# Softmax attention in a four-layer kernel on one core: the order of score and weighing matmuls, and the width of the maxima

## The chip, the cores and the metric

The kernel runs on one core of a Trainium2 chip. The metric is the device time of one execution in microseconds, median of the runs shown.

## What is computed

The reference is a chain of four layers on 1024 tokens of width 256: layer norm and softmax attention with 16 heads, a mixture of 8 experts, a linear attention with 16 heads, and a second mixture. The change touches the softmax attention alone. Cut to that:

```python
Xn = (X - mu) * rsqrt(var + 1e-5) * ln_w + ln_b        # 1024 x 256
q, k, v = split(Xn @ W_in)                              # 16 heads of 16 channels
q, k = rope(q), rope(k)                                 # the first 8 channels of each head
p = softmax(q @ k.T * 16 ** -0.5)                       # 16 x 1024 x 1024
context = p @ v                                         # then @ W_out, and the residual
```

## The kernel before, in words

Everything stands in one program. `attention_block` is its first block: a preparation (norm, transposes, tables of the rotary embedding, the projections of the first group of four heads and of all values), and then a loop over *units*. Each of the five engines runs its own instruction list in order, and semaphores tie them together.

A head's queries and keys lie in `q_stack` and `k_stack` as three float32 parts of 16 channels each, 48 rows, once on partitions 0 to 63 and once on 64 to 127 (`side` 0 and 1; `q_stack` holds another half of the queries on each side). Two more rows carry the negated row maximum, so that the second product comes out shifted.

- `score_rows_q(g, side)`: one matmul of 48 rows gives 128 queries x 512 keys. DVE (`row_maxima`) takes its maximum over the 512 keys. A head has 8 units (`NT`), of two such matmuls each, one per side; two halves of the keys are combined at the head's end (`whole_max`). Three banks of PSUM, `ps_q`, go round.
- POOL splits the maxima in two parts (`split_maxima`), PE turns them (`turn_max`), ACT copies them (`copy_max`), and SP's queue writes them into `q_stack`.
- `score_rows_k(kk, side)`: one matmul of 50 rows gives 128 keys x 512 queries, already shifted by the maximum; ACT takes the exponential into `probs` (`exp`). Three banks, `ps_k`, go round. It runs `K_LAG` = 13 units behind the maxima.
- `weigh(w)`: every second unit, two key tiles are weighed with the values (16 channels and a one for the sum, padded to 32 columns). Four matmuls of 128 x 32 weights and 512 moving columns write four strips of 32 partitions of one bank, `ps_ctx`: two strips for the even key tiles, two for the odd. In float32 each matmul is two instructions in the profile.
- When a head is done, ACT copies the bank (`copy_ctx`), PE turns its four blocks of 128 (`turn_ctx`, two and two) into `ps_turn`, ACT takes them (`take_ctx`), POOL adds the strips of even and odd tiles (`add_ctx`), DVE inverts the sums (`norm_ctx`), POOL multiplies (`weigh_ctx`).

The queries and keys of the other three groups of heads are projected inside the loop in 12 pieces of 256 columns (`project_piece`, units 0 to 11), copied by ACT (`copy_piece`), partly swapped by DMAs from SP's queue (`swap`), and prepared by POOL (`prepare`). `EARLY_AT` puts the projection of the first half of the contexts into the loop's tail. The functions `rotate`, `low`, `split_early` and all blocks behind attention are not edited.

A unit's order on PE is: `score_rows_q(g, 0)` with `score_rows_k(kk, 1)`, then perhaps a turn, then `score_rows_k(kk, 0)` with `score_rows_q(g, 1)`, then perhaps a piece, then on every second unit `weigh`. Two score matmuls on different sides run side by side in the array; such two are called a pair below.

## Time and profile before

| what | value |
|---|---|
| median of 3 runs | 1087.62 us |
| lowest, highest | 1085.27, 1093.72 us |
| the profiled execution, first to last instruction | 1084.3 us |
| mean granted clock of TensorE in it | 0.982 |
| PE busy | 1028.1 us (95%) |
| DVE busy | 787.5 us (73%) |
| ACT busy | 673.7 us (62%) |
| POOL busy | 507.1 us (47%) |

The profiled execution is given by its span; the fastest run stands 1.0 us above that and the median 3.3, which is what lies around a span and what runs differ by. PE's busy time counts matmuls as pipelined, so a high share says only that some matmul was under way. PE in a row is the matmul, PEld the load of its weights, SPq and ACTq are issues of DMAs. PEclk is the clock granted to TensorE, 1.00 being 2.4 GHz and 0.50 being 1.2 GHz.

### The profile page before, as it was taken

The page shows a single profiled execution, that of the slowest core. Times are in us where ns is not written, and L with a number is a line of the kernel's source. Part 1 is how long each engine was busy: PE and PEld are TensorE (multiplying, and loading weights), DVE is VectorE, ACT ScalarE, POOL GpSimd, SP SyncE. Part 2 cuts the span into 40 slices and gives each one's busy share as a digit, 9 for nine tenths or more (in the row PEclk, how much of TensorE's full clock was granted, in tenths as well). Part 3 has the DMA queues.
Part 4 walks back from the last instruction along what each step waited for, and adds up shares of the span by engine and source line. Part 5 has one row for each costly group of instructions (what it writes and reads, how often), then busy time and mean ns, then how long its engine had stood idle before and what let it go on. Part 6 is the DMA issues. An engine that isn't in the chain of part 4 may idle for free. (4 is left out here: it accounts for less than half of the span.)

```text
span 1084.3 us, 18619 instructions
## 1 busy us (share of the span) xinstructions
PE 1028.1 (95%) x6437; PEld 812.5 (75%) x6437; DVE 787.5 (73%) x1789; ACT 673.7 (62%) x1235; POOL 507.1 (47%) x457
## 2 busy tenths in 40 slices
PE   7999999989999997799999999999889999999997
PEld 5433333347888986699988998899789778888997
DVE  5789999836766856898999999998567465333843
ACT  4478888756544447788778878787456344333454
POOL 3252331114058561767686777777506000536544
PEclk9989999999999998899999999999899999999999
DMA  4533434205224300351113121221011123655100
GB/s 91 91 64 56 76 54 68 70 13 164 78 70 136 49 2 23 113 181 64 55 64 113 59 65 54 93 73 39 2 36 28 44 57 88 159 159 163 67 20 21
DMA packets 80633, 79.28 MB, mean 73 GB/s; under 512 B 29320, under 2 KB 67676, under 8 KB 80540
## 3 DMA queue, kind: packets, MB, share of 16 engines
q1 hardware_dynamic: 80228, 77.66, 27.0%
q8 instruction: 52, 0.85, 0.3%
q10 hardware_dynamic: 312, 0.43, 0.3%
q14 instruction: 41, 0.34, 0.1%
HBM read 65.51 MB, written 1.28 MB: 62 GB/s over the span
## 5 line engine op out<-in xcount | busy, mean ns | idle before, releaser
L682 ACT ACTIVATE attn_probs<-attn_rows_k 128x512 f32<-128x512 f32 x256 | 134.4, 605 | 37.2 <-PE attn_rows_k L533 37.0
L770 DVE TENSOR_REDUCE attn_row_max<-s_sum 128x1 f32<-128x512 f32 x171 | 111.8, 682 | 15.9 <-PE s_sum L519 13.3
L533 PE MATMUL attn_rows_k<-attn_q_stack,attn_k_stack 50*128 50x512 f32 x256 | 96.9, 465 | 5.7 <-ACT attn_probs L682 5.6
L2865 DVE TENSOR_TENSOR late_mids<-late_mids,late_bank 128x512 f32<-128x512 f32 (+1 forms) x50 | 34.4, 687 | 78.8 <-PE late_bank L67 75.8
L65 PE MATMUL late_bank<-net_x_part_low,late_w_T 128*128 128x512 f32 (+1 forms) x192 | 77.9, 406 | 0.0
L66 PE MATMUL late_bank<-net_x_part_low,late_w_T 128*128 128x512 f32 (+1 forms) x192 | 76.1, 396 | 0.0
L67 PE MATMUL late_bank<-net_x_part_low,late_w_T 128*128 128x512 f32 (+1 forms) x192 | 76.0, 396 | 0.0
L519 PE MATMUL s_sum<-attn_k_stack,attn_q_stack 48*128 48x512 f32 x171 | 72.8, 470 | 1.9 <-DMA attn_q_stack<-s_part 1.4
L1530 POOL TENSOR_TENSOR gold_mids<-gold_mids,s_later 128x512 f32<-128x512 f32 x32 | 51.9, 1659 | 46.2 <-DMA s_later<-gold_weights 46.2
L2770 ACT ACTIVATE late_mids<-late_bank 128x512 f32<-128x512 f32 (+1 forms) x50 | 29.9, 597 | 69.6 <-PE late_bank L67 69.5
L2966 POOL TENSOR_TENSOR late_mids<-late_mids,late_raw_w_T_last 128x512 f32<-128x512 f32 x22 | 29.8, 1378 | 89.7 <-DMA late_raw_w_T_last<-top_weights 89.7
L547 PE MATMUL attn_ctx<-attn_probs,attn_v 128*32 128x512 f32 x512 | 69.9, 619 | 0.0
L2119 DVE SCALAR_TENSOR_TENSOR lin_conv_q<-lin_pair,early_lin_taps,lin_conv_q 128x1021 f32<-128x1021 f32 (+2 forms) x48 | 61.5, 1281 | 7.3 <-ACT lin_conv_q L1979 4.0
L2119 DVE SCALAR_TENSOR_TENSOR lin_conv_k<-lin_pair,early_lin_taps,lin_conv_k 128x1021 f32<-128x1021 f32 (+2 forms) x48 | 61.4, 1279 | 2.7 <-issue 0.4
L770 DVE TENSOR_REDUCE attn_row_max<-attn_rows_q 128x1 f32<-128x512 f32 x85 | 57.9, 682 | 6.7 <-PE attn_rows_q L519 4.2
L519 PEld LDWEIGHTS s_sum<-attn_k_stack,attn_q_stack 48*128 48x128 f32 x171 | 30.3, 189 | 42.9 <-DVE attn_row_max L770 31.5
L533 PEld LDWEIGHTS attn_rows_k<-attn_q_stack,attn_k_stack 50*128 50x128 f32 x256 | 42.0, 189 | 24.2 <-ACT attn_probs L682 22.9
L1864 PE MATMUL lin_pair<-lin_probs,lin_v_rows 128*128 128x128 f32 x256 | 48.3, 282 | 4.3 <-DVE lin_state L2111 4.3
L1988 ACT ACTIVATE lin_normed_k<-lin_pair,lin_k_shift,lin_rstd_k 128x128 f32<-128x128 f32 x128 | 46.3, 473 | 0.6 <-DVE lin_k_shift L2091 0.6
L65 PE MATMUL late_bank<-late_down_T,late_w_T 128*128 128x256 f32 (+1 forms) x152 | 43.3, 285 | 1.8 <-POOL late_w_T L2565 1.8
L2755 ACT ACTIVATE late_w_T<-late_mids 128x256 fp32r<-128x256 f32 (+3 forms) x57 | 27.4, 488 | 27.4 <-PE late_bank L67 27.4
L1867 PE MATMUL lin_pair<-lin_q_dec,lin_state 128*128 128x128 f32 x224 | 44.3, 280 | 0.0
(459 smaller groups left out, 3491.9 us busy)
## 6 DMA issues: line engine op xcount, KB each, us to landing
lin_mix<-decay_sums SPq DMA_DIRECT2D x16, 512.0 KB, 3.8
lin_q_dec<-decay_sums SPq DMA_DIRECT2D x16, 512.0 KB, 5.3
s_later<-gold_weights SPq DMA_DIRECT2D x16, 256.0 KB, 3.6
attn_k_stack<-s_part SPq DMA_DIRECT2D x30, 128.0 KB, 3.5
s_raw_ring<-in_L_ffn_Wg SPq DMA_DIRECT2D x12, 256.0 KB, 2.8
s_raw_ring<-in_L_ffn_Wu SPq DMA_DIRECT2D x12, 256.0 KB, 3.1
attn_q_stack<-s_part SPq DMA_DIRECT2D x32, 64.0 KB, 2.4
gold_raw_w_down<-in_L_ffn_Wd SPq DMA_DIRECT2D x1, 2048.0 KB, 12.9
```

The source lines that it names most:

```text
L65: pe.matmul(out, w[0], x[0], start=start, stop=False)
L66: pe.matmul(out, w[0], x[1], start=False, stop=False)
L67: return pe.matmul(out, w[1], x[0], start=False, stop=stop)
L519: pe.matmul(ps_q[n % 3][:, :], q_stack[rows, h % SLOTS, r * P:(r + 1) * P], k_stack[rows, h % SLOTS, half * HALF:(half + 1) * HALF], start ...
L533: pe.matmul(ps_k[n % 3][:, :], k_stack[rows, h % SLOTS, t * P:(t + 1) * P], q_stack[rows, h % SLOTS, :], start=True, stop=True).then_inc(s ...
L547: i = pe.matmul(ps_ctx[j * VW:(j + 1) * VW, :], v[:, 2 * p + odd, h, :], probs[:, (2 * w + odd) % PB, b * HALF:(b + 1) * HALF], start=(p = ...
L682: act.activation(probs[:, kk % PB, side * HALF:(side + 1) * HALF], ps_k[n % 3][:, :], ACT.Exp)\
L770: dve.tensor_reduce(row_max[:, tile, half:half + 1], ps_q[n % 3][:, :], axis=AX, op=ALU.max)\
L1530: pool.tensor_tensor(out, out, weight[v % 4], ALU.mult).then_inc(weighted, 1)
L1864: i = pe.matmul(pair[2][:, cols], self.v_rows[h // 2 % 2][:, c, h % 2, :], self.probs[:, c, :], start=True, stop=(c == 0))
L1988: i = act.activation(self.normed[1][:, c, :], self.tiled[2][:, c, :], ACT.Identity, scale=self.rstd[1][:, c:c + 1], bias=self.k_shift[:, c ...
L2119: i = dve.scalar_tensor_tensor(self.conv[m][:, back:T], self.pair[pair][:, 0:T - back], self.taps[:, m, h, j:j + 1], self.conv[m][:, back: ...
```

## The change

The loop goes by *rounds* of two units, 4 per head, `ROUNDS_ALL` = 74 in all.

- **Maxima.** A tile of 128 queries x 1024 keys now fills two neighbouring banks, and DVE takes one maximum over the 1024 columns. Two pairs of banks alternate (a third serves in the first six rounds). `whole_max` and its combination are gone.
- **Order of the scores.** In a round PE does `score_rows_q` of side 0 for both halves of the keys, paired with `score_rows_k` of side 1 for two key tiles; then the same with the sides exchanged. Scores with the maximum lag 7 rounds, weighing 8.
- **Weighing.** `weigh(w, odd)` takes one key tile at a time: four matmuls of 32 weight columns and 256 moving columns, one for each quarter of the queries, into four strips of one half bank. It stands twice in a round, once behind each two pairs. Even and odd tiles accumulate in the same strips, so `add_ctx` is gone, `copy_ctx` copies 256 columns instead of 512, and one turn of two blocks replaces two turns.
- **Banks.** `ps_turn` is gone. The turns, the pieces and the exponentials share a ring of three banks, in an order computed beforehand (`ring`).
- **Pieces.** Six pieces of 512 columns instead of twelve of 256, one in each of rounds 0 to 5.
- **Queues.** The DMAs that write the rows of minus one and the first two swaps are issued by ACT instead of SP.

The core of the diff:

```diff
-        whole_max = [s.sb(f"whole_max{b}", [P, NT]) for b in range(2)]
+        row_max = [s.sb(f"row_max{b}", [P, NT]) for b in range(2)]
...
+        ctx_T = [s.sb(f"ctx_T{b}", [P, QUARTER]) for b in range(2)]
+        whole, inv = s.sb("whole", [P, 2, 2, 4, CW]), s.sb("inv", [P, 2, 2, 4])
...
+        ps_k = [ps_pair2[:, n * HALF:(n + 1) * HALF] for n in range(2)] + [s.ps("rows_k2", [P, HALF])[:, :]]
         ps_ctx = s.ps("ctx", [P, HALF])
-        ps_turn = s.ps("turn", [P, HALF])
-        turn_max_ps = ps_turn[0:MROWS * NT, 0:P]
-        piece_ps = ps_turn[:, 0:HALF // 2]
+        sums = ps_ctx[:, 0:QUARTER]
...
         inner = probs[:, 0:2, :].rearrange("p a (c d) -> p (a c) d", d=D)
         rope_rows = [probs[:, 2 + n, :].rearrange("p (c d) -> p c d", c=NT) for n in range(2)]
...
+        ROUNDS = NT // 2
+        Q_ROUNDS = ROUNDS * NH
+        K_LAG, W_LAG = 7, 8
+        MAX_LAG, COPY_LAG, TURN_LAG, NORM_LAG = ROUNDS, W_LAG + ROUNDS, W_LAG + ROUNDS + 1, W_LAG + ROUNDS + 2
+        ROUNDS_ALL = ROUNDS * (NH - 1) + TURN_LAG + 1
+        PIECES = 6
...
-        EARLY_AT = {UNITS + 1: ("turn", 0), UNITS + 2: ("rows", 0), UNITS + 3: ("rows", 1),
-                    UNITS + 4: ("project", 0), UNITS + 5: ("project", 1), UNITS + 7: ("turn", 1)}
-        def units():
-            for g in range(SLOTS_ALL * NT):
-                kk = g - K_LAG
-                w = kk - W_LAG
-                yield (g // NT, g % NT, g if g < UNITS else None, kk if 0 <= kk < UNITS else None,
-                       w // 2 if w % 2 and 0 < w < UNITS else None)
+        EARLY_AT = {Q_ROUNDS: (("turn", 0),), Q_ROUNDS + 1: (("rows", 0), ("rows", 1)),
+                    Q_ROUNDS + 2: (("project", 0), ("project", 1)), Q_ROUNDS + 3: (("turn", 1),)}
+        def rounds():
+            for q in range(ROUNDS_ALL):
+                k, w = q - K_LAG, q - W_LAG
+                yield (q, q if q < Q_ROUNDS else None, k if 0 <= k < Q_ROUNDS else None, w if 0 <= w < Q_ROUNDS else None)
...
+        def tile_bank(n):
+            return n % 3 if n < 2 * PIECES else n % 2
...
+        K_SIDES = ((0, 1), (1, 1), (0, 0), (1, 0))
+        ring = []
+        for q, _, k, _ in rounds():
+            if k is not None:
+                ring += [("exped", 4 * k + 1), ("exped", 4 * k + 2)]
+            if head_at(q, TURN_LAG) is not None:
+                ring.append(("ctx_taken", head_at(q, TURN_LAG) + 1))
+            if k is not None:
+                ring += [("exped", 4 * k + 3), ("exped", 4 * k + 4)]
+            if q < PIECES:
+                ring.append(("piece_copied", q + 1))
+            if head_at(q, MAX_LAG) is not None:
+                ring.append(("max_copied", head_at(q, MAX_LAG) + 1))
...
+        def ring_bank(job):
+            n = ring.index(job)
+            return ps_k[2 if n < ring_first else (n - ring_first) % 3]
...
-                def project_piece(n, r):
-                    first = n % 2 * HALF + r * HALF // 2
...
+                def project_piece(n):
+                    if n == 0:
                         pe.wait_ge(rest_loaded, 64)
-                    else:
-                        pe.wait_ge(piece_copied, 2 * n + r)
-                    if 2 * n + r == FIRST_TURN:
-                        pe.wait_ge(max_copied, 1)
-                    project(piece_ps, w_qk[:, :, 1 + n // 2, :], slice(first, first + HALF // 2)).then_inc(pieced, 1)
+                        pe.wait_ge(v_copied, 4)
+                    out = ring_free(("piece_copied", n + 1))
+                    project(out, w_qk[:, :, 1 + n // 2, :], slice(n % 2 * HALF, (n % 2 + 1) * HALF)).then_inc(pieced, 1)
...
-                def score_rows_q(g, side):
-                    h, u = divmod(g, NT)
-                    r, half = divmod(u, 2)
-                    if u == 0 and side == 0:
...
+                    if half == 0 and tile_before[n] is not None:
+                        pe.wait_ge(maxed, tile_before[n] + 1)
                     rows = slice(side * SIDE_ROWS, side * SIDE_ROWS + QROWS)
-                    pe.matmul(ps_q[n % 3][:, :], q_stack[rows, h % SLOTS, r * P:(r + 1) * P],
+                    pe.matmul(ps_tile[tile_bank(n)][:, half * HALF:(half + 1) * HALF],
+                              q_stack[rows, h % SLOTS, r * P:(r + 1) * P],
                               k_stack[rows, h % SLOTS, half * HALF:(half + 1) * HALF], start=True, stop=True)\
                         .then_inc(scored_q, 1)
...
-                def score_rows_k(kk, side):
-                    h, t = divmod(kk, NT)
-                    if t == 0 and side == 1:
...
-                    n = 2 * kk + 1 - side
-                    if n >= 3:
-                        pe.wait_ge(exped, n - 2)
+                            pe.wait_ge(maxed, 2 * PIECES)
+                    out = ring_free(("exped", 4 * k + n + 1))
                     rows = slice(side * SIDE_ROWS, side * SIDE_ROWS + QROWS + MROWS)
-                    pe.matmul(ps_k[n % 3][:, :], k_stack[rows, h % SLOTS, t * P:(t + 1) * P], q_stack[rows, h % SLOTS, :],
+                    t = 2 * r + odd
+                    pe.matmul(out, k_stack[rows, h % SLOTS, t * P:(t + 1) * P], q_stack[rows, h % SLOTS, :],
                               start=True, stop=True).then_inc(scored_k, 1)
...
-                def weigh(w):
-                    h, p = divmod(w, NT // 2)
-                    pe.wait_ge(exped, 4 * (w + 1))
-                    if p == 0 and h >= 1:
+                def weigh(w, odd):
+                    h, r = divmod(w, ROUNDS)
+                    t = 2 * r + odd
+                    pe.wait_ge(exped, 4 * w + 3 + odd)
+                    if t == 0 and h >= 1:
                         pe.wait_ge(ctx_copied, h)
-                    for odd in range(2):
-                        for b in range(2):
-                            j = 2 * b + odd
-                            i = pe.matmul(ps_ctx[j * VW:(j + 1) * VW, :], v[:, 2 * p + odd, h, :],
-                                          probs[:, (2 * w + odd) % PB, b * HALF:(b + 1) * HALF],
-                                          start=(p == 0), stop=(p == NT // 2 - 1))
+                    for j in range(4):
+                        i = pe.matmul(sums[j * VW:(j + 1) * VW, :], v[:, t, h, :],
+                                      probs[:, (2 * w + odd) % PB, j * QUARTER:(j + 1) * QUARTER],
+                                      start=(t == 0), stop=(t == NT - 1))
                     i.then_inc(summed, 1)
...
-                for n, u, g, kk, w in units():
-                    if u == U_MAX and 1 <= n <= NH:
-                        turn_max(n - 1)
-                    if g is not None:
-                        score_rows_q(g, 0)
-                    if kk is not None:
-                        score_rows_k(kk, 1)
-                    if u in U_CTX and 3 <= n:
-                        turn_ctx(n - 3, U_CTX.index(u))
-                    if kk is not None:
-                        score_rows_k(kk, 0)
-                    if g is not None:
-                        score_rows_q(g, 1)
-                    if n * NT + u in PIECE_AT:
-                        project_piece(*PIECE_AT[n * NT + u])
+                for n, q, k, w in rounds():
+                    if k is None and q is not None:
+                        for half in range(2):
+                            for side in range(2):
+                                score_rows_q(q, side, half)
+                    if k is not None:
+                        for p in range(2):
+                            if q is not None:
+                                score_rows_q(q, 0, p)
+                            score_rows_k(k, p)
                     if w is not None:
-                        weigh(w)
-                    if n * NT + u in EARLY_AT:
-                        what, j = EARLY_AT[n * NT + u]
+                        weigh(w, 0)
+                    if head_at(n, TURN_LAG) is not None:
+                        turn_ctx(head_at(n, TURN_LAG))
+                    if k is not None:
+                        for p in range(2):
+                            if q is not None:
+                                score_rows_q(q, 1, p)
+                            score_rows_k(k, 2 + p)
+                    if w is not None:
+                        weigh(w, 1)
+                    if n < PIECES:
+                        project_piece(n)
+                    if head_at(n, MAX_LAG) is not None:
+                        turn_max(head_at(n, MAX_LAG))
+                    for what, j in EARLY_AT.get(n, ()):
                         {"turn": turn_early, "rows": add_rows, "project": project_early}[what](j)
-                for half in range(2):
-                    turn_ctx(NH - 1, half)
...
-                    act.activation(plain_half(n)[:, r * HALF // 2:(r + 1) * HALF // 2], piece_ps, ACT.Copy)\
-                        .then_inc(piece_copied, 1)
+                    act.activation(plain_half(n), ring_bank(("piece_copied", n + 1)), ACT.Copy).then_inc(piece_copied, 1)
...
                 def copy_ctx(h):
-                    act.wait_ge(summed, NT // 2 * (h + 1))
+                    act.wait_ge(summed, NT * (h + 1))
...
-                    act.activation(ctx_T[h % 2][:, :], ps_ctx[:, :], ACT.Copy).then_inc(ctx_copied, 1)
+                        act.wait_ge(ctx_turned, h - 1)
+                    act.activation(ctx_T[h % 2][:, :], sums, ACT.Copy).then_inc(ctx_copied, 1)
...
-                def exp(kk):
-                    if kk >= PB:
-                        act.wait_ge(summed, (kk - PB) // 2 + 1)
-                    for side in (1, 0):
-                        n = 2 * kk + 1 - side
-                        act.wait_ge(scored_k, n + 1)
-                        act.activation(probs[:, kk % PB, side * HALF:(side + 1) * HALF], ps_k[n % 3][:, :], ACT.Exp)\
-                            .then_inc(exped, 1)
+                    view = ring_bank(("ctx_taken", h + 1))[:, 0:2 * P].rearrange("p (c s w) -> p c s w", c=2, s=4)
+                    act.activation(whole[:, h % 2, :, :, :], view[:, :, :, 0:CW], ACT.Copy).then_inc(ctx_taken, 1)
+                def exp(k, n):
+                    odd, side = K_SIDES[n]
+                    if n < 2 and 2 * k + odd >= PB:
+                        act.wait_ge(summed, 2 * k + odd - PB + 1)
+                    act.wait_ge(scored_k, 4 * k + n + 1)
+                    act.activation(probs[:, (2 * k + odd) % PB, side * HALF:(side + 1) * HALF],
+                                   ring_bank(("exped", 4 * k + n + 1)), ACT.Exp).then_inc(exped, 1)
...
-                for n, u, g, kk, w in units():
-                    if u == U_MAX and 1 <= n <= NH:
-                        copy_max(n - 1)
-                    if u == U_COPY and 2 <= n < NH + 2:
-                        copy_ctx(n - 2)
-                    if kk is not None:
-                        exp(kk)
-                    if u == U_TAKE and 3 <= n:
-                        take_ctx(n - 3)
-                    if n * NT + u in PIECE_AT:
-                        copy_piece(*PIECE_AT[n * NT + u])
-                    if n == 0:
-                        norm_x(u)
-                take_ctx(NH - 1)
+                stack_ones()
+                for n, q, k, w in rounds():
+                    if head_at(n, COPY_LAG) is not None:
+                        copy_ctx(head_at(n, COPY_LAG))
+                    if k is not None:
+                        exp(k, 0)
+                        exp(k, 1)
+                    if head_at(n, TURN_LAG) is not None:
+                        take_ctx(head_at(n, TURN_LAG))
+                    if k is not None:
+                        exp(k, 2)
+                        exp(k, 3)
+                    if n < PIECES:
+                        copy_piece(n)
+                        if n < 2:
+                            act.wait_ge(piece_copied, n + 1)
+                            swap_rows(act, n)
+                    if n < ROUNDS:
+                        norm_x(2 * n)
+                        norm_x(2 * n + 1)
+                    if head_at(n, MAX_LAG) is not None:
+                        copy_max(head_at(n, MAX_LAG))
...
-                def row_maxima(g):
-                    h, u = divmod(g, NT)
...
-                    for side in range(2):
-                        n, tile = 2 * g + side, r + side * NT // 2
-                        dve.wait_ge(scored_q, n + 1)
-                        dve.tensor_reduce(row_max[:, tile, half:half + 1], ps_q[n % 3][:, :], axis=AX, op=ALU.max)\
-                            .then_inc(maxed, 1)
-                    if u == NT - 1:
-                        if h >= 2:
-                            dve.wait_ge(max_split, h - 1)
-                        dve.drain()
-                        dve.tensor_tensor(whole_max[h % 2][:, :], row_max[:, :, 0], row_max[:, :, 1], ALU.max)\
-                            .then_inc(whole_ready, 1)
-                        dve.drain()
+                def row_maxima(q, side):
+                    h, r = divmod(q, ROUNDS)
+                    n = 2 * q + side
+                    if r == 0 and side == 0 and h >= 2:
+                        dve.wait_ge(max_split, h - 1)
+                    dve.wait_ge(scored_q, 4 * (q + 1) if side or q < K_LAG else 4 * q + 2)
+                    tile = r + side * ROUNDS
+                    dve.tensor_reduce(row_max[h % 2][:, tile:tile + 1], ps_tile[tile_bank(n)][:, :], axis=AX, op=ALU.max)\
+                        .then_inc(maxed, 1)
```

## Rows read from the trace of the kernel before

**Rows 1.** stage windows; length, busy us (instructions) of each engine, PEclk, DMA share, GB/s

```profile
50.94:61.18 10.24, 10.17 (x39) 3.92 (x39) 6.93 (x13) 5.46 (x12) 6.04 (x7) 0.50 0.14 26
...
72.80:83.76 10.96, 10.63 (x71) 4.02 (x70) 10.12 (x18) 9.06 (x21) 6.58 (x9) 1.00 0.44 80
...
52.30:208.72 156.42, 151.72 (x963) 56.84 (x963) 142.32 (x251) 126.30 (x265) 44.43 (x78) 0.97 0.39 68
28.02:52.30 24.28, 22.81 (x87) 12.40 (x88) 19.45 (x32) 11.36 (x26) 6.02 (x7) 0.97 0.54 93
208.72:235.64 26.92, 23.19 (x133) 9.54 (x131) 9.61 (x15) 17.37 (x35) 5.42 (x12) 0.99 0.00 1
```

**Rows 2.** the table of waits, 72.8 to 204.4 us

```profile
PEld s_sum L519 <- DVE attn_row_max L770: 22.6, 30, 0.8
```

**Rows 3.** PE's timeline: start us, us, engine, line, operation

```profile
170.18 0.40 PE L519 MATMUL attn_rows_q<-attn_k_stack,attn_q_stack 48*128 48x512 f32 x1
...
170.51 0.44 PE L505 MATMUL attn_turn<-net_ident,attn_ctx_T 128*128 128x128 f32 x2
...
170.89 0.49 PE L519 MATMUL s_sum<-attn_k_stack,attn_q_stack 48*128 48x512 f32 x1
171.31 1.07 PE L547 MATMUL attn_ctx<-attn_probs,attn_v 128*32 128x512 f32 x8
172.30 0.49 PE L519 MATMUL s_sum<-attn_k_stack,attn_q_stack 48*128 48x512 f32 x1
...
172.64 0.40 PE L519 MATMUL attn_rows_q<-attn_k_stack,attn_q_stack 48*128 48x512 f32 x1
```

**Rows 4.** passes of 512 and 256 columns: ns min/median/max

```profile
L447 PE MATMUL attn_rows_k<-net_raw_x_part,attn_w_qk x8: 592/592/697, 11.5 to 17.4; 128*128 128x512 f32 x8
...
L468 PE MATMUL attn_rows_k<-s_raw_w_v,net_raw_x_part x16: 379/379/379, 23.0 to 26.2; 128*128 128x256 f32 x16
```

**Rows 5.** PE's timeline, a turn behind a lone score matmul

```profile
216.11 0.49 PE L533 MATMUL attn_rows_k<-attn_q_stack,attn_k_stack 50*128 50x512 f32 x1
216.53 0.44 PE L505 MATMUL attn_turn<-net_ident,attn_ctx_T 128*128 128x128 f32 x2
```

**Rows 6.** DVE on PSUM, 512 and 1024 columns: ns min/median/max

```profile
L770 DVE TENSOR_REDUCE attn_row_max<-s_sum x171: 641/681/693, 28.6 to 209.3; 128x1 f32<-128x512 f32 x171
...
L2099 DVE TENSOR_TENSOR lin_probs<-lin_pair,lin_mix x16: 1210/1211/1217, 457.0 to 781.2; 128x1024 f32<-128x1024 f32 x16
```

**Rows 7.** ACT: four exponentials in the timeline; the 256-column copy, a group's line

```profile
172.93 2.07 ACT L682 ACTIVATE attn_probs<-attn_rows_k 128x512 f32<-128x512 f32 x4 [0.63 <-PE attn_rows_k L533]
...
L656 ACT ACTIVATE s_later<-attn_turn 128x256 f32<-128x256 f32 x8 | 3.1, 385 | 7.4 <-PE attn_turn L447 7.4
```

**Rows 8.** PE's timeline, a piece's projection and the next pair

```profile
30.05 1.13 PE L447 MATMUL attn_turn<-net_raw_x_part,attn_w_qk 128*128 128x256 f32 x4
31.11 0.50 PE L519 MATMUL s_sum<-attn_k_stack,attn_q_stack 48*128 48x512 f32 x1
```

**Rows 9.** DMA issues in the timeline, on ACT's and on SP's queue

```profile
21.88 2.56 ACTq L233 DMA_DIRECT2D attn_k_stack<-s_part  x4
...
33.53 5.40 SPq L255 DMA_DIRECT2D s_raw_ring<-s_raw_ring  x4
```

**Rows 10.** PE's timeline, weighings at the beginning and in the tail

```profile
53.53 1.93 PE L547 MATMUL attn_ctx<-attn_probs,attn_v 128*32 128x512 f32 x8
...
61.87 1.06 PE L547 MATMUL attn_ctx<-attn_probs,attn_v 128*32 128x512 f32 x8
...
217.33 1.07 PE L547 MATMUL attn_ctx<-attn_probs,attn_v 128*32 128x512 f32 x8
...
221.79 0.64 PE L547 MATMUL attn_ctx<-attn_probs,attn_v 128*32 128x512 f32 x4
...
231.19 1.06 PE L547 MATMUL attn_ctx<-attn_probs,attn_v 128*32 128x512 f32 x8
```

**Rows 11.** POOL's timeline, the addition of the last context

```profile
234.14 0.43 POOL L375 TENSOR_TENSOR attn_whole<-attn_whole 128x136 f32<-128x136 f32 x1 [1.21 <-ACT attn_whole L674]
```

168 lines of the change are left out of this document (80 added, 88 removed).

## The prediction

> **What bounds the kernel now.** I read the stage windows first [rows 1]. Only the attention block is edited; its loop begins at 28.02 us and the block ends at 235.64. Everything before and behind is the same code, so the question is what the 207.6 us between become. I cut them where the change's rounds can be laid on the old units: 24.28 us until unit 16 (the first that weighs values), 156.42 for units 16 to 127, 26.92 for the tail in which maxima are finished and scores and weighing run out. In the middle piece one head (8 units, 4 weighings) takes 10.96 us; DVE is busy 10.12 of it, ACT 9.06, PE 10.63. The shares don't decide between DVE and PE, the order on PE does.
>
> In the table of waits PE's weight loads are held longest by DVE's maxima, 22.6 us in 12 heads [rows 2], which looks like a DVE bound. The timeline of PE says otherwise [rows 3]: weighing starts at 171.31, the next pair of score matmuls (one on rows 0 to 63, one on rows 64 to 127, side by side) at 172.30, the next at 172.64. That is PE's own work without a gap: 0.99 us for a weighing, 0.34 for the first pair behind it. A pair whose weights were loaded under its predecessor shows 0.40 us and one whose weights were not shows 0.49; a turn of a context follows the first kind after 0.33 (170.18 to 170.51), and the weighing follows the second kind after 0.42 (170.89 to 171.31). The two transposes take 0.37 or 0.38 until the next pair. A pair behind a pair loaded ahead should take 0.23, the 0.34 less the 0.1 of waiting for weights. Added up, 0.99 + 0.34 + 0.23 + 0.33 + 0.38 + 0.42 = 2.69 us for two units with a turn in them, and 4 x 2.74 is the 10.96 of the head. So PE, in program order, is the bound, and DVE and ACT fill about 92% and 83% beside it.
>
> **The change part by part.**
>
> *Maxima.* Before, 16 reductions of 512 columns per head, 0.68 us each [rows 6], then a combining maximum with two drains. After, 8 of 1024 columns. The nearest row is another DVE operation that reads 1024 columns of PSUM, 1.21 us [rows 6]; 0.68 plus 512 more columns gives the same. If none overlaps the next, DVE needs 2 x 1.21 = 2.42 us per round of two units; old ones overlap (16 x 0.68 is 10.9, and DVE is busy 10.12 of a head with the small operations in it), by some 0.07 each, which makes 2.28, and 9.3 with the reciprocal for a head. DVE falls from 10.12 to 9.3, but it isn't the bound: by itself this is worth nothing beyond the slack it gives PE.
>
> *Scores.* Four pairs per round, as before. They were four in a row; now they are two and two, with a weighing behind each two.
>
> *Weighing.* Before, one visit per two units: 4 strips x 2 passes of 512 columns, 0.99 us until PE does something else. Now two visits, each 4 strips x 2 passes of 256 columns. A float32 pass of 256 columns takes 379 ns where one of 512 takes 592 [rows 4], 0.213 less, so a visit costs 0.99 - 2 x 0.213 = 0.56. Two cost 1.12 where one cost 0.99. The streamed columns are equal; the extra 0.13 and the extra change from scores to weighing and back are the price of the finer interleaving.
>
> *The round on PE.* Half a round is: first pair 0.34 (weights not loaded ahead, because a weighing stands before it), second pair, weighing 0.56. The second pair's weights can be loaded under the first. What follows such a pair starts after 0.33; what follows one not loaded ahead starts after 0.42, be it a weighing (170.89 to 171.31) or a turn (216.11 to 216.53) [rows 3, 5]. Every weighing of the old trace stands behind the second kind, so its price behind the first kind isn't shown; between 0.33 and 0.43 I take 0.33, because the turn shows both prices and the weighing shares the one that it has. Half: 1.23, round: 2.46.
>
> *Once per head.* One turn of two transposes instead of two turns: 0.37 (it stood twice, 0.74). The transpose of the maxima: 0.21, as before. Two new couplings: the first weighing of a head waits for the copy of the last context. The last pass ends about 0.05 us into the round, ACT is free at 0.4, a 256-column copy is 0.385 [rows 7], so it is through at 0.8 and PE wanted it at 0.66: 0.15 lost. And the transposes now take banks from the ring of three that the exponentials use: behind the turn of the maxima the second score matmul waits for an exponential that ends 0.49 us into the round instead of one that ends before it: 0.2 lost. Head: 4 x 2.46 + 0.37 + 0.21 + 0.35 = 10.77 us, against 10.96 now.
>
> *Does ACT keep up?* The exponential starts 0.62 us behind its matmul (172.30 to 172.93) and four take 2.07 [rows 3, 7]. With matmuls at 0, 0.34, 1.23 and 1.57 of a round the exponentials start at 0.62, 1.12, 1.85 and 2.35. The first weighing of the next round, at 2.46 + 0.66, needs the third (ends at 2.45), the second weighing needs the fourth (2.95) at 2.46 + 1.90; the second score matmul's weights at 2.46 + 0.1 need the bank of the third. Margins are 0.1 us and more, so ACT hides, barely. Its smaller jobs (copy of 256 instead of 512 columns, 136 instead of 272 elements taken) help, and so does POOL's missing addition; none of them is on the path except at the very end.
>
> *First piece, 28.02 to unit 16.* Before, a unit was a pair, a wait and four passes of a 256-column projection, 1.06 us until the next pair (30.05 to 31.11 [rows 8]), and 16 units took 24.28. After, a 512-column piece once a round: 0.34 + 0.33 + (1.06 + 4 x 0.213 = 1.91) = 2.58 per two units; rounds 6 and 7 have none and go by DVE's 2.28 and its waits, which makes about 20 for eight rounds if nothing else held them. But ACT now issues what SP issued: the minus ones and two swaps, two DMAs each, in rounds 0 and 1. A row of ACT has four issues in 2.56 us, 0.64 each; the same swaps took SP 5.40 for four, 1.35 each [rows 9]. The piece's single bank isn't free until ACT has copied it, so ACT's 1.3 to 2.7 us per swap, with the copy and two normalisations, paces rounds 1 to 3. Walking it through gives unit 16 at 49.7 with the short issues and 52.7 with the long ones, against 52.30: between -2.6 and +0.4, I take -1.1.
>
> *Middle, rounds 8 to 63.* 14 x 10.77 = 150.8. The clock adds to it: TensorE stood at 0.50 of its clock (1.2 GHz) from 50.94 to 61.18 [rows 1], after units in which PE had only scattered score pairs; the weighings at 53.53 and 61.87 [rows 10], two periods of 2.70 apart by rights, lie 8.34 apart: 2.9 us lost. The new rounds 6 and 7 are as thin, so I keep 2.9. 153.7, against 156.42: -2.7.
>
> *Tail.* Seven rounds with scores at 2.46 = 17.2; then turns, copy stalls and the early projection. Its matmuls fill two periods like the one from 217.33 to 221.79, 4.46 us where 2.7 is the rule [rows 10], so 3.5 for both; its two turns, which had stood in waits for ACT, cost 1.1, the turns and couplings of the last heads 1.5; together 6.1. The last weighings and the end of the last head take 3.5: from the last old weighing at 231.19 to 235.64 it was 4.45 [rows 10], now without the addition on POOL (0.43 and its wait [rows 11]), with a copy shorter by 0.2, two transposes fewer, and one more half weighing ahead. 26.8 against 26.92: -0.1. The pipeline's drain becomes cheaper per pair but no longer hides the turns in waits for ACT.
>
> Sum: -1.1 - 2.7 - 0.1 = -3.9. The profiled span is 1084.3; the median shown is 3.3 above it, the fastest run 1.0. I apply the change to the median: **1083.7 us**. A change below about 1% can't be told from none here.
>
> **The rivals.**
>
> *A: each change from scores to weighing costs the full 0.42 to 0.43 (slower).* Mechanism: the second pair of each half round is followed by a weighing that finds the array still draining, whatever was loaded ahead. For it: all weighings of the trace cost that. Against it: the turn's 0.33. Price: 0.1 x 2 x 64 rounds = 12.8 us, head 11.2, total 1096.5. It is slower than before as soon as the switch costs over 0.36, 0.03 above my price. Chance 0.22. The Trainium skill, TensorEngine Tiling (Array Packing), Key Properties, states that changing the tiling mode, and not just the tile, drains TensorE. Here scores use half the rows and weighing a quarter of the columns, so the change doubles such switches, and by that rule A would be the outcome; the trace agrees that a switch costs 0.1 to 0.2 more than a pair behind a pair, and doesn't show whether early weights hide part of it.
>
> *B: the couplings vanish and the beginning is quick (faster).* Head 4 x 2.46 + 0.58 = 10.42, short DMA issues (-2.6), and no clock drop (-2.9): 145.9 - 156.4 - 2.6 - 0.1 = -13.2, 1074.4; with the clock drop 1077.3. For it: the couplings are worked out from margins of 0.1. Against: PE is as thin at the beginning. Chance 0.17.
>
> *C: the ring binds.* One score matmul late by a tenth is not loaded ahead, costs 0.1 more, and delays the next exponential; with 0.1 in every round +6.4, and a clock that stays at 1.2 GHz for another stretch in the ACT-paced rounds +2: 1086 to 1093. Chance 0.13.
>
> *D: DVE was the bound after all.* Then a round would be 2.3 to 2.35 us, a head 9.4, and the total near 1065. The start of weighing to the start of the next pair being 0.99 in every period, whatever DVE does, speaks against it. Chance 0.03.
>
> **How the numbers follow.** The forecast has 0.45, with 1079 to 1089 as its own range. The range for 8 in 10 reaches from B to A: 1075 to 1098. Faster by over 1% (below 1076.7): 0.17, two thirds of B, D and an edge of the forecast. Slower by over 1% (above 1098.5): 0.15, half of A and a bit of C. Within: 0.68.
>
> **What would show it.** In the new trace: one reduction of 1024 columns at 1.2 us and DVE idle about 0.2 us per round, waiting for PE. A weighing to the next pair 0.56. Second pair to weighing 0.33 (right) or 0.43 (A). Head period 10.8 (10.4 B, 11.2 A, 9.4 D). Unit 16's place between 49.7 and 52.7, with PE idle in front of pieces, released by ACT copies. The prediction fails if the 256-column visit isn't 0.56, if a score matmul waits on ACT in ordinary rounds, or if the clock is at 1.2 GHz in a stretch where it wasn't.

## The result, and the profile of the changed kernel

The changed kernel took 1084.79 us (median of 10 executions, 1077.89 to 1177.66), the kernel before 1089.07 us on the same chip (10 executions, 1085.27 to 1093.72). The ratio is 0.9941, 95% interval [0.9918, 0.9965]: faster by 0.6%, less than the 1% that I had called the limit of what can be told, yet outside no change. Executions over 1.5% above the fastest of their kernel, here 1101.74 and 1177.66, are left out of this and the later ratios; the median of the other eight is 1083.02. The profiled execution of the changed kernel took 1086.34 us, its span is 1084.4, no shorter than the 1084.3 of the kernel before.

The stage windows of the changed kernel, cut at the same places as [rows 1]: one head in the steady part; rounds 8 to 11; rounds 8 to 63; the beginning up to round 8; the tail. Columns as in [rows 1].

```profile
79.44:90.08 10.64, 10.53 (x105) 4.13 (x101) 9.80 (x10) 9.34 (x20) 6.52 (x8) 1.00 0.45 82
50.51:68.11 17.60, 17.60 (x98) 5.69 (x98) 10.51 (x9) 9.45 (x19) 6.02 (x7) 0.50 0.34 60
...
50.51:207.22 156.71, 155.39 (x1385) 59.79 (x1385) 137.55 (x126) 130.44 (x266) 40.37 (x67) 0.94 0.39 69
28.44:50.51 22.07, 18.54 (x61) 6.94 (x62) 17.77 (x16) 9.43 (x19) 6.01 (x7) 0.98 0.56 100
207.22:233.52 26.30, 24.30 (x196) 11.17 (x192) 7.70 (x12) 17.49 (x36) 1.96 (x6) 1.00 0.00 1
```

A head is 10.64 us where it was 10.96, and yet the middle piece is no shorter (156.71 against 156.42). The second row says why: rounds 8 to 11 took 17.6 us at a granted clock of 0.50, PE busy in all of it. The attention loop and its tail are 2.5 us shorter than before; it begins 0.4 us later (28.44 against 28.02), and the code behind, which is the same, took 850.88 instead of 848.66, which is scatter: in the kernels below it took 849 to 854.

The page's row of granted clock, a digit for each fortieth of the span:

```profile
PEclk9979999999999998899999999999999999999999
```

PE's timeline of one ordinary round of the changed kernel (start us, us, engine, line, operation), which answers to [rows 3]:

```profile
150.18 0.49 PE L538 MATMUL attn_rows_q<-attn_k_stack,attn_q_stack 48*128 48x512 f32 x1
...
150.51 0.39 PE L538 MATMUL attn_rows_q<-attn_k_stack,attn_q_stack 48*128 48x512 f32 x1
...
150.84 0.64 PE L567 MATMUL attn_ctx<-attn_probs,attn_v 128*32 128x256 f32 x8
151.41 0.49 PE L538 MATMUL s_sum<-attn_k_stack,attn_q_stack 48*128 48x512 f32 x1
...
151.74 0.39 PE L538 MATMUL s_sum<-attn_k_stack,attn_q_stack 48*128 48x512 f32 x1
...
152.07 0.64 PE L567 MATMUL attn_ctx<-attn_probs,attn_v 128*32 128x256 f32 x8
152.64 0.49 PE L538 MATMUL attn_rows_q<-attn_k_stack,attn_q_stack 48*128 48x512 f32 x1
```

Read the differences of the starts: 0.33 or 0.34 from pair to pair, 0.33 from the second pair to the weighing, 0.57 from the weighing to the next pair, 1.23 for half a round, 2.46 for a round (150.18 to 152.64), with nothing idle between. The same view where a head ends holds what comes once per head:

```profile
153.87 0.49 PE L538 MATMUL s_sum<-attn_k_stack,attn_q_stack 48*128 48x512 f32 x1
...
154.20 0.39 PE L538 MATMUL s_sum<-attn_k_stack,attn_q_stack 48*128 48x512 f32 x1
...
154.71 0.64 PE L567 MATMUL attn_ctx<-attn_probs,attn_v 128*32 128x256 f32 x8
155.28 0.49 PE L538 MATMUL attn_rows_q<-attn_k_stack,attn_q_stack 48*128 48x512 f32 x1
...
156.51 0.28 PE L516 MATMUL attn_rows_k<-net_ident,attn_max_tok 128*16 128x128 f32 x1
156.72 0.50 PE L538 MATMUL s_sum<-attn_k_stack,attn_q_stack 48*128 48x512 f32 x1
...
157.41 0.64 PE L567 MATMUL attn_ctx<-attn_probs,attn_v 128*32 128x256 f32 x8
157.98 0.44 PE L523 MATMUL attn_rows_k<-net_ident,attn_ctx_T 128*128 128x128 f32 x2
158.35 0.49 PE L538 MATMUL attn_rows_q<-attn_k_stack,attn_q_stack 48*128 48x512 f32 x1
```

The weighing at 154.71 stands 0.51 behind its pair instead of 0.33: 0.18 for the copy of the last context. The half with the turn of the maxima costs 0.21 more (156.51 to 156.72), the next half is 1.26 instead of 1.23 (156.72 to 157.98), the turn of the context takes 0.37. So four rounds of 2.46 and these: 9.84 + 0.18 + 0.21 + 0.03 + 0.37 = 10.63.

DVE in one head, grouped by line; columns as in the groups of [rows 7]:

```profile
L810 DVE TENSOR_REDUCE attn_row_max<-attn_rows_q 128x1 f32<-128x1024 f32 x5 | 6.1, 1225 | 0.5 <-PE attn_rows_q L538 0.4
L810 DVE TENSOR_REDUCE attn_row_max<-s_sum 128x1 f32<-128x1024 f32 x4 | 4.9, 1220 | 0.3 <-PE s_sum L538 0.2
```

A reduction of 1024 columns takes 1.22 us, and what DVE waits for is PE. Eight of them are 9.8 us, as much as DVE's busy time in the head, so little of one overlaps the next. (Nine lie wholly or in part in the window, eight belong to a head.)

The beginning, PE's projection of a piece and ACT's DMA issues, which answer to [rows 8, 9]:

```profile
29.10 1.98 PE L473 MATMUL attn_rows_k<-net_raw_x_part,attn_w_qk 128*128 128x512 f32 x4
31.02 0.49 PE L538 MATMUL attn_rows_k<-attn_k_stack,attn_q_stack 48*128 48x512 f32 x1
...
31.75 1.64 ACTq L279 DMA_DIRECT2D s_raw_ring<-s_raw_ring  x2
...
35.04 1.16 ACTq L279 DMA_DIRECT2D s_raw_ring<-s_raw_ring  x2
35.06 1.98 PE L473 MATMUL attn_rows_k<-net_raw_x_part,attn_w_qk 128*128 128x512 f32 x4 [0.65 <-ACT s_raw_ring L681]
...
48.16 0.50 PE L538 MATMUL s_sum<-attn_k_stack,attn_q_stack 48*128 48x512 f32 x1 [1.35 <-DVE attn_row_max L810]
```

A piece holds PE for 1.92 us, an issue on ACT is 0.58 to 0.82 us, and PE waits 0.65 and 0.15 for ACT's copies (at 35.06 and 37.87) and 1.35 for DVE at round 7, just before the clock falls at 49.6.

### The profile page after: what moved, and what is told of

Read it like the earlier page. It is cut to its first block and busy times, and to the rows that moved or that the text cites. A ratio compares the mean times of both kernels' runs of the same rounds, so it can differ in the third digit from the quotient of the medians.

```text
span 1084.4 us, 19328 instructions
## 1 busy us (share of the span) xinstructions
PE 1030.0 (95%) x6893; PEld 813.3 (75%) x6893; DVE 781.1 (72%) x1645; ACT 675.8 (62%) x1229; POOL 500.7 (46%) x441
## 5 line engine op out<-in xcount | busy, mean ns | idle before, releaser
L706 ACT ACTIVATE attn_probs<-attn_rows_k 128x512 f32<-128x512 f32 x256 | 138.9, 595 | 33.5 <-PE attn_rows_k L554 30.6
L810 DVE TENSOR_REDUCE attn_row_max<-s_sum 128x1 f32<-128x1024 f32 x62 | 75.6, 1220 | 15.8 <-PE attn_rows_q L538 7.4
L567 PE MATMUL attn_ctx<-attn_probs,attn_v 128*32 128x256 f32 x1024 | 85.4, 407 | 1.4
L810 DVE TENSOR_REDUCE attn_row_max<-attn_rows_q 128x1 f32<-128x1024 f32 x62 | 75.9, 1225 | 12.5 <-PE attn_rows_q L538 9.3
L404 POOL TENSOR_SCALAR attn_max_tok<-attn_row_max 128x8 fp32r<-128x8 f32 x16 | 3.2, 199 | 137.3 <-DVE attn_row_max L810 137.2
L567 PEld LDWEIGHTS attn_ctx<-attn_probs,attn_v 128*32 128x32 f32 x1024 | 20.9, 110 | 49.1 <-ACT attn_probs L706 33.8
L538 PE MATMUL s_sum<-attn_k_stack,attn_q_stack 48*128 48x512 f32 x124 | 47.6, 465 | 3.0 <-DVE attn_row_max L810 1.6
L538 PE MATMUL attn_rows_q<-attn_k_stack,attn_q_stack 48*128 48x512 f32 x124 | 47.4, 463 | 0.3 <-DVE attn_row_max L810 0.3
## 6 DMA issues: line engine op xcount, KB each, us to landing
gold_raw_w_down<-in_L_ffn_Wd SPq DMA_DIRECT2D x1, 2048.0 KB, 12.3
```

The lines of the kernel that those rows point to most:

```text
L538: pe.matmul(ps_tile[tile_bank(n)][:, half * HALF:(half + 1) * HALF], q_stack[rows, h % SLOTS, r * P:(r + 1) * P], k_stack[rows, h % SLOTS, ...
L567: i = pe.matmul(sums[j * VW:(j + 1) * VW, :], v[:, t, h, :], probs[:, (2 * w + odd) % PB, j * QUARTER:(j + 1) * QUARTER], start=(t == 0), ...
L706: act.activation(probs[:, (2 * k + odd) % PB, side * HALF:(side + 1) * HALF], ring_bank(("exped", 4 * k + n + 1)), ACT.Exp).then_inc(exped, 1)
L810: dve.tensor_reduce(row_max[h % 2][:, tile:tile + 1], ps_tile[tile_bank(n)][:, :], axis=AX, op=ALU.max)\
```

## The experiments

Each ratio is taken against executions of the kernel before on the same chip. The experiments ran on three chips, so they are compared by their ratios, not by their medians.

**Are the maxima over 1024 columns worth anything?** In the changed kernel each maximum is taken as before, over two halves of 512, and combined once per head.

```diff
-                    dve.tensor_reduce(row_max[h % 2][:, tile:tile + 1], ps_tile[tile_bank(n)][:, :], axis=AX, op=ALU.max)\
-                        .then_inc(maxed, 1)
+                    for half in range(2):
+                        i = dve.tensor_reduce(half_max[:, tile, half:half + 1],
+                                              ps_tile[tile_bank(n)][:, half * HALF:(half + 1) * HALF], axis=AX, op=ALU.max)
+                    i.then_inc(maxed, 1)
```

> The changed kernel with one part undone: DVE takes each tile's maximum as two reductions of 512 columns, and combines them once per head, as before the change; order, weighing, banks and ring stay. My theory (PE's order is the bound): a head in the middle stays at 10.6 to 10.8 us, since DVE needs about 2.45 us of a round of 2.46, so at most 0.2 us per head is lost and the whole is within 3 us of the changed kernel. Rival (the wide maxima brought the gain, DVE is the bound): the head goes back to 10.9 or more and the total to that of the kernel before.

Measured: 1082.88 us, ratio 0.9937 [0.9908, 0.9966]; three of the ten executions took 1169.53, 1169.86 and 1189.55 us. The window of one head of this kernel:

```profile
79.44:90.08 10.64, 10.53 (x107) 4.13 (x99) 10.13 (x19) 9.33 (x20) 4.98 (x8) 1.00 0.41 60
```

DVE is busy 10.13 us of the head instead of 9.80, and the head is the same 10.64. DVE doesn't set the time at either load; rival D falls.

**Is the interleaving in two halves needed?** Both weighings of a round behind its fourth pair.

```diff
-                    if w is not None:
-                        weigh(w, 0)
                     if head_at(n, TURN_LAG) is not None:
...
                     if w is not None:
+                        weigh(w, 0)
                         weigh(w, 1)
```

> The changed kernel with both weighings of a round behind its fourth pair, so that there is one change from scores to weighing per round instead of two; maxima, banks and widths stay. My theory (what gains is that a score matmul never waits for an exponential, because a weighing stands between): the matmuls alone would sum to 2.2 us, but the fourth score matmul must wait for the first exponential, about 1.25 us into the round, and the round becomes 2.7 us, the head near 10.9, the total near the kernel before. Rival (switches between score and weighing are what counts, the Trainium skill's rule of the drain): the round becomes 2.3 us, by DVE, the head 9.4 and the total 18 us shorter than the changed kernel.

Measured: 1093.04 us, ratio 1.0046 [1.0028, 1.0063], a head 11.51 us. The expected 10.9 had left out what comes once per head. PE's timeline of this kernel, one round:

```profile
150.07 0.50 PE L538 MATMUL s_sum<-attn_k_stack,attn_q_stack 48*128 48x512 f32 x1
...
150.41 0.62 PE L554 MATMUL attn_rows_k<-attn_q_stack,attn_k_stack 50*128 50x512 f32 x2
150.64 0.62 PE L538 MATMUL attn_rows_q<-attn_k_stack,attn_q_stack 48*128 48x512 f32 x2
151.35 0.50 PE L554 MATMUL attn_rows_k<-attn_q_stack,attn_k_stack 50*128 50x512 f32 x1
151.77 1.07 PE L567 MATMUL attn_ctx<-attn_probs,attn_v 128*32 128x256 f32 x16
152.78 0.49 PE L538 MATMUL s_sum<-attn_k_stack,attn_q_stack 48*128 48x512 f32 x1
```

A round is 2.71 (150.07 to 152.78). The saved switch is there (the four strips of both key tiles in 1.01 us), but the round's last score matmul needs a bank of the ring of three and starts at 151.35; its partner on the other rows, the second of the two counted at 150.64, had started at 150.88. Its weight load waited 0.52 us for an exponential:

```profile
151.34 0.18 PEld L554 LDWEIGHTS attn_rows_k<-attn_q_stack,attn_k_stack 50*128 50x128 f32 x1 [0.52 <-ACT attn_probs L705]
```

It is also followed after 0.42 instead of 0.33, as an unprepared matmul is. The halves pay for themselves by giving the ring time. That is rival C's mechanism, seen where it does bind.

**Who issues the first DMAs?** The minus ones and the first two swaps go back to SP.

```diff
-                stack_ones()
...
-                        if n < 2:
-                            act.wait_ge(piece_copied, n + 1)
-                            swap_rows(act, n)
```

> The changed kernel with the DMAs of the rows of minus one and of the first two swaps issued by SP again. If ACT's issues pace rounds 1 to 3, the waits of PE for copies of pieces (0.65 and 0.15 us) vanish and unit 16 begins 0.5 to 1 us earlier than at 50.51. If SP's queue then delays the stacked rows of head 2 and the maxima of head 0, PE or DVE waits for a DMA instead and the beginning is no shorter. Either way within 2 us in total, unless the stretch at 1.2 GHz that begins near 49.6 us moves.

Measured: 1080.74 us, ratio 0.9919 [0.9891, 0.9948]; round 8 begins at 49.46, 1.05 earlier than in the changed kernel. Of this 0.31 is a loop that begins earlier, at 28.13 instead of 28.44; the beginning itself is 0.74 shorter (21.33 against 22.07), and the two waits of PE for ACT's copies, 0.65 and 0.15, are gone. Its profiled execution, though, took 1142.17 us, and is the clearest trace of what had cost the changed kernel its middle piece. Windows of it:

```profile
67.68:85.89 18.21, 18.21 (x101) 5.98 (x99) 9.91 (x9) 9.62 (x20) 6.20 (x8) 0.50 0.27 48
...
100.00:200.00 100.00, 100.00 (x548) 32.73 (x548) 54.40 (x50) 53.06 (x106) 15.90 (x28) 0.50 0.22 36
```

The granted clock was 0.50, 1.2 GHz, from 50.0 us for 153.6 us without a break, while PE was busy in every microsecond of it. A head took 18.21 us instead of 10.63, so each microsecond at 1.2 GHz loses 1 - 10.63 / 18.21 = 0.42 us: 64 us for this stretch, against a distance of 61 from this kernel's median. The other five executions took 1075.56 to 1083.40 us.

**Does the thin beginning bring the clock down?** Three float32 matmuls of 512 columns, whose results nobody reads, fill PE in rounds 6 and 7.

```diff
+                def keep_warm(times):
+                    for _ in range(times):
+                        pe.matmul(ps_ctx[:, :], ident[:, :], xT[:, 0, 0:HALF], start=True, stop=True)
...
+                    keep_warm({6: (1, 1), 7: (1, 0)}.get(n, (0, 0))[0])
                     if w is not None:
                         weigh(w, 0)
...
+                    keep_warm({6: (1, 1), 7: (1, 0)}.get(n, (0, 0))[1])
                     if w is not None:
                         weigh(w, 1)
```

> The changed kernel with three float32 matmuls of 512 columns added that nothing reads, two in round 6 and one in round 7, where PE has little to do (0.85 us each). If the stretch at 1.2 GHz from 49.6 to 70.1 us comes of those thin rounds, it vanishes or shrinks: the first four weighing rounds take 10.6 us instead of 17.6 and the total falls by up to 7 us, less 0.5 for the added work. If it comes of something else (the score matmuls themselves, which use half the rows), the clock falls just the same and the total rises by about 0.5 us.

Measured: 1080.79 us (1078.56 to 1082.68), ratio 0.9930 [0.9907, 0.9953]. The windows of rounds 8 to 11 and 16 to 63:

```profile
51.00:61.48 10.48, 10.46 (x99) 3.94 (x96) 10.07 (x9) 9.39 (x19) 6.08 (x7) 1.00 0.14 24
...
72.11:200.33 128.22, 126.41 (x1193) 49.63 (x1189) 117.62 (x109) 112.00 (x229) 30.14 (x55) 1.00 0.41 73
```

Rounds 8 to 11 take 10.48 us where the changed kernel's trace had 17.60, the clock is full throughout, and the matmuls themselves cost 0.5 (round 8 at 51.00). In the ratio the gain over the changed kernel's 0.9941 is not told apart from none.

The thin rounds don't bring the clock down each time, though. The kernel with maxima in halves has no such matmuls, and PE idles in its rounds 6 to 8 as in the changed kernel (1.41, 0.40 and 0.56 us against 1.35, 0.33 and 0.23), yet in its trace the clock stays up. Two windows of it:

```profile
44.00:50.50 6.50, 4.17 (x18) 1.63 (x16) 6.27 (x11) 2.37 (x5) 2.75 (x3) 1.00 0.49 69
49.60:70.08 20.48, 19.81 (x188) 7.58 (x184) 19.82 (x36) 17.82 (x37) 8.31 (x11) 1.00 0.35 61
```

Of the eight traces without the unread matmuls seven show a fall between 49.6 and 52.0 us, this one none; of the four with them, here and below, none shows it there. Both edits together:

> The changed kernel with both edits that helped: ones and swaps issued by SP, and the three matmuls that nothing reads in rounds 6 and 7. If they add up: unit 16 begins near 49.9, no stretch at 1.2 GHz before the end of attention, a median of 1079 to 1080 and no execution above 1085. If the two work on the same idle time of PE, it stays at the 1080.8 of the extra matmuls alone.

Measured: 1079.37 us (1076.97 to 1081.67), ratio 0.9912 [0.9887, 0.9938], the lowest median of all these kernels, though its ratio isn't told apart from the 0.9930 of the matmuls alone; beginning 21.76 (28.22 to 49.98), middle 149.30, tail 26.32 us. In the 12 executions of these two kernels none is above 1083 us. In the 26 of the changed kernel, of the one with maxima in halves and of the one with SP's issues, none of which has the matmuls, six are above 1100. If the matmuls changed nothing, all six would still miss those 12 about once in twelve times, so this alone doesn't show that they prevent long executions.

**The same matmuls in the kernel before**, in units 12, 13 and 14:

```diff
+                    keep_warm({12: 1, 13: 1, 14: 1}.get(n * NT + u, 0))
                     if w is not None:
                         weigh(w)
```

> The kernel before with the same three unread float32 matmuls of 512 columns, one in each of units 12, 13 and 14. Nothing else is changed. The kernel before lost 2.9 us to the stretch at 1.2 GHz that begins at 50.94, and the matmuls themselves cost up to 0.6 us each of PE time that it had free there. Theory 1 (the stretch is the consequence of thin score pairs, in both kernels, and costs the changed kernel more): no stretch at 1.2 GHz between 50 and 200 us, the execution about 2 to 3 us faster than the kernel before, ratio 0.997 to 0.999, while the same matmuls gave the changed kernel about 4 us of its median. Theory 2 (the matmuls help by something else, or the old kernel isn't touched by them): no difference, ratio 1.000 or above.

Measured: 1086.85 us, ratio 0.9974 [0.9957, 0.9991]. Its middle piece:

```profile
53.64:207.38 153.74, 148.43 (x964) 56.09 (x961) 142.50 (x251) 126.47 (x265) 44.33 (x78) 1.00 0.39 69
```

153.74 against 156.42: the old kernel had lost 2.7 us to its stretch at 1.2 GHz, and the beginning got 1.15 longer. This is also the fair pair for the change itself, both at full clock: middle 153.74 against 149.33 with the changed order, -4.4 us, and by the ratios 0.9930 against 0.9974, 4.8 us, in all. The two don't quite fit: in these two traces the beginning is also 2.9 shorter (22.58 against 25.43) and the tail 0.6, 7.9 in all, while each ratio is known to about 2.5 us either way. And the second half of theory 1 isn't seen: by the ratios the matmuls gave the old kernel 2.8 us (0.9974) and the changed one 1.2 (0.9941 to 0.9930), the latter within noise.

**What is the next bound, and what does PE's load do to the clock?** Only even key tiles are weighed: the second weighing of each round, and with it half of the values, is left out.

```diff
                     if w is not None:
-                        weigh(w, 1)
+                        pass
```

> The changed kernel weighing only the even key tiles (half of the values are left out), so a round has one weighing, behind its first two pairs. It asks which limit stands next behind PE. PE's matmuls then sum to about 0.34 + 0.33 + 0.56 + 0.34 + 0.24 = 1.81 us. My theory: DVE's two reductions bound the round at 2.28 us, the head at 9.2 to 9.4 us, so DVE lies 1.3 us per head below the changed kernel's 10.63. Rival (ACT with its exponentials and copies is next, or the ring): above 9.6 us.

Measured: 1131.25 us, ratio 1.0383 [1.0342, 1.0424] (two executions, 1130.79 and 1131.70), less work and 4% slower. The clock was 0.50 from 49.6 us for 211.6 us; a head took 14.23 us, PE busy nearly all of it. So this run said nothing of the next bound at full clock. With the three unread matmuls (half of the values again left out):

> The changed kernel with only the even key tiles weighed (the second weighing of each round and with it half of the values is left out, and one round of the weighing's sums is its last), and with the three unread matmuls of e4 in rounds 6 and 7. Without them the same kernel stood at 1.2 GHz for 211 us. Theory 1 (PE's order bounds the changed kernel, DVE is next): if the clock is at 2.4 GHz, a head falls from 10.63 to about 9.4 to 9.8 us, DVE busy for nearly all of it, and the attention loop ends some 12 to 17 us earlier than at e4's. Theory 2 (DVE, ACT or the ring of three already bound it): a head stays at 10.4 or more. Whether the matmuls at the beginning are enough is open: PE then has 0.56 us less work in each round; if the clock is at 1.2 GHz all through, the head is 14.2 again and the kernel above 1125 us.

Measured: 1123.78 us, ratio 1.0331 [1.0288, 1.0374]. Windows of it, two heads next to each other before the clock fell and one after:

```profile
50.74:60.59 9.85, 9.25 (x67) 3.77 (x65) 9.38 (x9) 9.03 (x18) 6.05 (x7) 1.00 0.11 19
60.59:70.85 10.26, 9.65 (x68) 4.14 (x68) 9.19 (x10) 8.91 (x20) 2.95 (x5) 1.00 0.59 102
100.00:114.23 14.23, 14.17 (x69) 6.82 (x69) 9.59 (x9) 9.21 (x20) 0.77 (x3) 0.50 0.30 44
```

At full clock, two passes of four strips fewer per round make a head 9.85 and 10.26 us instead of 10.48 and 10.63: PE's order was the bound, but by little: with 0.57 us less per round (2.3 per head) only 0.4 to 0.6 come off. Behind PE, DVE and ACT are close (9.2 to 9.4 and 8.9 to 9.0). How much of the 10.26 is each of them and the ring isn't settled: two heads were seen, no more. Then, at 74.8 us, the clock fell to 1.2 GHz for 180.9 us. In the head before PE had been busy for 9.65 of 10.26 us, but from 70.85 to 74.80 only for 2.22 of 3.95, and when the clock fell it stood idle, from 73.43 on, until POOL had split the maxima:

```profile
75.28 0.38 PE L516 MATMUL attn_rows_k<-net_ident,attn_max_tok 128*16 128x128 f32 x1 [1.85 <-POOL attn_max_tok L406]
```

So this fall, too, follows idle time of PE, a wait that the unread matmuls in rounds 6 and 7 don't fill. The same wait took 1.31 us in the kernel with maxima in halves and 0.47 in the full order with the matmuls, and there the clock stayed up.

**Is the changed kernel slower to recover?** In both kernels PE waits once in the middle for POOL, which fills an unused tile.

```diff
+                        for n in range(5):
+                            i = pool.memset(idle_rows[:, :], 0.0)
+                            pool.drain()
...
+                    if n == 40:
+                        pe.wait_ge(resumed, 1)
```

> The changed kernel with PE made to wait once in the middle, after round 40, for five fills of POOL (some 5 to 10 us). It asks how long TensorE stays at 1.2 GHz once it is there. My theory: the new order doesn't bring the clock back by itself as readily as the old one; a stretch of 20 us or more at 1.2 GHz follows, in some executions one of over 100 us, and heads in it take 18.2 us. Rival: the clock comes back within about 10 us as it does in the old kernel, and the long stretches seen have another cause.

> The kernel before with the same pause of PE, in unit 83. My theory: the clock falls here too and comes back after about 10 us, as after 50.94, so that the total rises by the pause and 3 to 4 us. Rival: it stays down as long as in the changed kernel with the pause, and the order has nothing to do with it.

Measured: 1094.83 us with the changed order, 1.0044 [1.0020, 1.0068], and 1097.82 with the old one, 1.0080 [1.0051, 1.0108]. PE's first matmul behind the pause and the stretch at 1.2 GHz (from 142.9 and from 151.0 us), first of the changed order:

```profile
144.49 0.79 PE L545 MATMUL s_sum<-attn_k_stack,attn_q_stack 48*128 48x512 f32 x1 [5.57 <-POOL attn_idle_rows L444]
```

```profile
142.90:160.00 17.10, 15.51 (x86) 5.18 (x86) 8.06 (x8) 8.19 (x16) 2.42 (x7) 0.50 0.21 29
```

and of the old one:

```profile
153.15 0.79 PE L526 MATMUL s_sum<-attn_k_stack,attn_q_stack 48*128 48x512 f32 x1 [3.65 <-POOL attn_idle_rows L414]
```

```profile
151.00:157.80 6.80, 4.65 (x18) 1.60 (x18) 2.65 (x5) 2.17 (x4) 2.26 (x4) 0.50 0.61 87
```

The changed order stood at 1.2 GHz for 17.1 us, the old one for 6.8; the heads lost 12.3 us (22.07 + 11.48 - 2 x 10.64) against 5.8 (16.71 - 10.95), the pauses included. The 17.1 us are less than the 20 that I had expected at least, and the 6.8 less than the 10. But the pauses came out unequal, 5.57 us of idle PE against 3.65, because the weighing before it ends later in the old order. With one trace each they don't settle whether it is the order or the pause, and the beginnings of the same two traces go the other way: near 51 us the changed order stood at 1.2 GHz for 3.4 us and the old one for 13.7.

```profile
50.80:54.20 3.40, 3.40 (x23) 0.91 (x20) 2.56 (x3) 1.93 (x4) 2.87 (x4) 0.50 0.14 25
```

```profile
52.00:65.60 13.60, 13.60 (x53) 4.55 (x52) 8.61 (x15) 6.78 (x14) 6.04 (x7) 0.50 0.30 43
```

What does tell the orders apart is the number of long executions. Of 64 executions of the kernel before, taken beside all these runs, the longest took 1094.53 us; of the 26 of the changed order named above six took over 1100. Spread by chance over the 90, all six would fall on the changed order less than once in a thousand times. With the pause it is one of ten (1116.78) with the changed order and, of four with the old, none above 1100.20. The kernel with both weighings behind the fourth pair had none above 1097.67 in eleven, too few to say that the halves are what matters.

## Why the prediction was right, and where it was not

The time came out at 1084.79 for a forecast of 1083.7, within the forecast's own range of 1079 to 1089. Against the median of 1089.07 measured beside it, the change is -4.3, or -6.05 without the two executions above 1100 us (by the ratio -6.4); the forecast was -3.9. That it came so near is in part luck: the sum hides errors of opposite sign, in the steady head and the beginning one way and in the clock the other, and the two profiled executions don't differ at all (-2.2, +0.3 and -0.6 for the three pieces, +0.4 ahead of them and +2.2 behind).

*The round on PE: right.* Weighing to pair 0.57 (forecast 0.56), second pair to weighing 0.33 and not rival A's 0.43, round 2.46. A's condition is thereby answered: in this trace a weighing behind a pair with early weights starts after 0.33. (A's own head was added up wrong: 0.1 for each of 8 switches on 10.77 is 11.57, not 11.2; its total of 1096.5 is right.) The Trainium skill, TensorEngine Tiling (Array Packing), Key Properties, states that changing the tiling mode drains TensorE. In this case such a drain is no more than the 0.1 us between 0.33 and the 0.23 after which a pair starts behind a pair loaded ahead (150.41 to 150.64 in the timeline of the kernel with both weighings together); whether early loading hides more of it isn't shown.

*What bounds the kernel: right.* Taking 0.33 us of DVE's work per head away or giving it back changes nothing. DVE's own load was mis-sized, without effect: 9.80 us per head for a forecast of 9.3, which had counted on reductions that overlap.

*Couplings once per head: mis-sized.* Copy 0.18 (forecast 0.15); ring 0.03 (forecast 0.2), except in one head of the trace, the one whose end is shown above, where behind the turn of the context another 0.18 is lost (a head of 10.81). Hence a head of 10.63 instead of 10.77, which is 14 x 0.14 = 2.0 us. At full clock the middle piece was 149.3 where I had 150.8, a gain of 4.4 for 2.7; 0.5 of the 149.3 is a wait of PE for POOL at 74.8 us that the forecast doesn't have.

*The clock: the step that failed.* "The new rounds 6 and 7 are as thin, so I keep 2.9" took the loss over from the old trace. The stretch begins where I said (49.6 us, old 50.94) but lasted 20.48 us in this trace instead of 10.24: rounds 8 to 15 took 28.9 us (17.59 + 11.33) against 21.1 with the unread matmuls (10.48 + 10.63), a loss of 7.8. The profiled execution thus lost 4.9 us more than forecast, and the middle piece gained nothing. No single figure would have been right, for the amount changes from execution to execution: in the traces without unread matmuls the stretch that begins near 50 us lasted 10.2 and 13.7 us in the old order, and 0, 3.4, 20.5 and 153.6 in the changed one (with maxima in halves, with the pause, as it is, and with SP's issues). The share of the span at 1.2 GHz is twice what the mean granted clock lacks to 1: 0.987 in the execution of 1077.89 us leaves 28 us, 0.974 in that of 1089.18 leaves 57, and 11.3 us of time for these 28.5 us more is 0.40 for each, near the 0.42 of a head. How much of them lies in the attention isn't known, since the code behind it stood at 1.2 GHz for 17 to 46 us in the twelve traces. Rival C held a stretch more at 1.2 GHz, at 2 us, together with a ring that binds; the first came, the second didn't.

*Beginning: right in its means, too small.* Piece to pair 1.92 (1.91), ACT's issues 0.58 to 0.82 each, around the short end of what I had bounded (0.64). Length -2.2 instead of -1.1. ACT does pace it, which SP's issuing shows by the 0.74 us it gives back.

*Tail: -0.6 instead of -0.1,* not taken apart by an experiment.

*Rival B* is half true: couplings of 0.21 instead of 0.35 (it had none), a beginning 2.2 shorter (2.6), and in some executions no long stretch at 1.2 GHz: the two of 1077.89 us have a mean clock of 0.987, and lie 0.6 above where B was (1074.4 to 1077.3).

## What to carry to other kernels

When PE's order is the bound, write down the starts of one period and price each kind of neighbour (pair behind pair, weighing behind pair, pair behind weighing) from the old trace: the finer interleaving was right to 0.01 us per half round, while margins of 0.1 us against other engines were not worth adding up as losses. A stretch at 1.2 GHz is not a constant to carry over: it lasted 0 to 153.6 us in one and the same place, and it can be worth more than the edit. A median hides that: with the two long ones counted, the mean of the ten executions is 1094.1 us for the changed kernel and 1089.4 for the kernel before. Try a few unread matmuls where PE idles just before a steady loop: here three cost 0.5 us and the profiled rounds 8 to 11 got 7.1 us back. In the ratio that is 0.9930 against 0.9941, not told apart, since most executions of the changed kernel lose less than its profiled one; but of twelve executions with them none was above 1083 us, and three of ten of the changed kernel were above 1089. Look for every wait of PE, too: a later one, for POOL, preceded the fall in the kernel with half of the weighing left out.
